# Second wide attention layer: the first pair's transposed exponentials copied out of PSUM by ScalarE instead of VectorE

## The reference

```
q = rope((decoder_query @ Wq).reshape(B, Sq, 16, 64)) / sqrt(64)
k = rope((encoder_key_value @ Wk).reshape(B, Skv, 16, 64))
v = (encoder_key_value @ Wv).reshape(B, Skv, 16, 64)
scores = einsum('bqhd,bkhd->bhqk', q, k);  scores = where(mask, scores, -1e9)
attn = softmax(scores);  out = einsum('bhqk,bkhd->bqhd', attn, v).reshape(B, Sq, 1024) @ Wo
x = decoder_query + out;  then a layer norm of x
```

## Time and profile before

| what | us |
|---|---|
| median of 3 runs | 2019.13 (2017.56 to 2023.05) |
| the profiled execution's own time | 2018.0 |
| its span in the trace | 2016.1 |

### The profile page before, as it was taken

One profiled execution on the slowest core, in us unless ns is written; L12 is line 12 of the kernel. 1 busy time (PEld: TensorE's weight loads), 2 busy tenths in 40 slices (PEclk: granted clock), 3 DMA queues, 4 the chain that ended last, 5 costly groups with the idle time before them and its releaser, 6 DMA issues. The chain is left out here.

```text
span 2016.1 us, 50639 instructions
## 1 busy us (share of the span) xinstructions
PE 1899.3 (94%) x18654; PEld 1644.1 (82%) x18654; DVE 1443.3 (72%) x3163; ACT 1291.5 (64%) x3129; POOL 598.3 (30%) x740
## 2 busy tenths in 40 slices
PE   7799998999999999999999999999999998898998
PEld 6677777898888888888887887887888877777786
DVE  5688875546555555555589899999999974677775
ACT  4577776556656565566566666666666663777775
POOL 3233230000000000000076677777776730000000
PEclk8899999999999999999999999999999997999999
DMA  5444442201101001000102000000100002443441
GB/s 159 151 148 142 125 134 68 92 25 61 28 21 28 17 22 29 21 24 21 42 25 59 20 20 26 23 23 18 30 22 19 22 14 69 126 128 120 128 134 56
DMA packets 111774, 123.02 MB, mean 61 GB/s; under 512 B 45964, under 2 KB 101420, under 8 KB 111532
## 3 DMA queue, kind: packets, MB, share of 16 engines
q1 hardware_dynamic: 111244, 119.26, 20.0%
q10 hardware_dynamic: 288, 0.51, 0.1%
HBM read 82.29 MB, written 37.45 MB: 59 GB/s over the span
## 5 line engine op out<-in xcount | busy, mean ns | idle before, releaser
L645 ACT ACTIVATE L_P<-PS,MX 100x361 f32<-100x361 f32 x512 | 252.6, 565 | 126.8 <-DVE MX L775 126.8
L775 DVE TENSOR_REDUCE MX<-PS 100x2 f32<-100x722 f32 x256 | 219.9, 901 | 52.9 <-PE PS L525 52.7
L537 PE MATMUL PP<-CON,L_P 100*128 100x100 f32 x1536 | 180.8, 254 | 26.7 <-DVE L_PT L782 22.1
L1544 ACT ACTIVATE wide_V<-PJ 105x512 f32<-105x512 f32 (+1 forms) x143 | 84.1, 594 | 165.5 <-PE PJ L1375 165.5
L1579 ACT ACTIVATE wide_P<-wide_P,MX 100x361 f32<-100x361 f32 x256 | 149.9, 588 | 59.6 <-DVE MX L1717 57.8
L537 PEld LDWEIGHTS PP<-CON,L_P 100*128 100x128 f32 x1536 | 148.5, 142 | 47.4 <-ACT L_P L645 33.9
L1579 ACT ACTIVATE wide_P<-PS,MX 100x361 f32<-100x361 f32 x256 | 140.4, 563 | 70.0 <-DVE MX L1722 70.0
L1442 PEld LDWEIGHTS PS<-CON,wide_P 100*128 100x128 f32 x1536 | 159.6, 140 | 29.4 <-ACT wide_P L1579 8.1
L1442 PE MATMUL PS<-CON,wide_P 100*128 100x100 f32 x1536 | 176.9, 250 | 4.1 <-ACT wide_P L1579 3.1
L1938 POOL TENSOR_TENSOR wide_AC<-wide_T,wide_COSM 128x362 f32<-128x362 f32 x128 | 133.2, 1041 | 155.2 <-issue 155.2
L1455 PEld LDWEIGHTS PP<-wide_PT,wide_V 128*64 128x64 f32 (+1 forms) x3072 | 137.0, 137 | 38.1 <-issue 38.0
(11 more groups left out here) (252 smaller groups left out, 5627.2 us busy)
## 6 DMA issues: line engine op xcount, KB each, us to landing
strips<-L_KS SPq DMA_DIRECT2D x256, 90.5 KB
L_KA<-strips SPq DMA_DIRECT2D x64, 362.0 KB, 3.1
wide_RB<-recip SPq DMA_DIRECT2D x128, 100.0 KB, 2.8
C<-ctx_t SPq DMA_DIRECT2D x32, 361.0 KB, 3.1
kept<-L_CTH SPq DMA_DIRECT2D x16, 361.0 KB, 4.8
kept<-L_CTL SPq DMA_DIRECT2D x16, 361.0 KB, 5.4
L_CTH<-kept SPq DMA_DIRECT2D x16, 361.0 KB, 4.2
L_CTL<-kept SPq DMA_DIRECT2D x16, 361.0 KB, 5.0
```

The source lines that it names most:

```text
L537: last = nc.tensor.transpose(PPB[:, n, SQ * t:SQ * t + SQ], P[:, (4 * g + 2 * i + n) % 8, 128 * t:128 * t + 128], ident[0:SQ, 0:SQ])
L645: nc.scalar.activation(P[:, (4 * g + j) % 8, 0:SK], PSB[0:SQ, j, 0:SK], ACT.Exp, bias=MX[:, s % 2, 4 * q + j:4 * q + j + 1], scale=1.0).th ...
L775: nc.vector.tensor_reduce(MX[:, s % 2, 4 * q + 2 * i:4 * q + 2 * i + 2], PSB[0:SQ, 2 * i:2 * i + 2, 0:SK], AX.X, ALU.max, negate=True).the ...
L1544: nc.scalar.activation(V[0:r, 1024 * t + 512 * part:1024 * t + 512 * part + 512], bank(key)[0:r, 0:512], ACT.Copy).then_inc(Z["v_taken"], 1)
```

## The change

In layer 2 (slots of `s >= B`) the copy of the first pair's transposes leaves VectorE and is made by ScalarE, right behind its two copies of K tiles to `wide_T` and ahead of the second `wide_KH`. Layer 1 keeps its division. Each copy still counts up the semaphore that TensorE waits for, `unloaded_first` for the first pair.

```diff
                         act.wait_ge(Z["turned"], 2 * g + 2)
                         if g >= 4:
                             act.wait_ge(Z["weighed"], g - 1)
-                        nc.scalar.activation(PT[:, 2:4, :], PSB[:, 2:4, 0:KV_TILES * SQ], ACT.Copy).then_inc(Z["unloaded_second"], 1)
+                        n = 2 * (g % 2)
+                        nc.scalar.activation(PT[:, n:n + 2, :], PSB[:, n:n + 2, 0:KV_TILES * SQ], ACT.Copy).then_inc(unloaded(g)[0], 1)
@@ ScalarE's loop over slots @@
                         for key in first:
                             job(key)
+                        if B <= s < NS:
+                            unload(2 * G)
                         for key in turns_of(G - 1)[1:]:
                             rotated_high(key)
@@ VectorE's loop over slots @@
                         for key in first:
                             job(key)
-                        if s < NS:
+                        if s < B:
                             unload(2 * G)
```

## The result

The changed kernel took 2011.84 us in the median of 11 runs (2006.65 to 2016.52), the kernel before 2020.17 (2014.8 to 2029.46, 11 runs). The ratio is 0.9957, 95% interval 0.9941 to 0.9972: faster by 0.4%, where I had forecast 2021.5, no change or slower. Two executions of later runs, at 6086 and 4449 us, were far off all others of their kernels and are left out of the ratios. The profiled execution has a span of 2014.0 us.

A forecast was written before the change was run, and what follows sets the result against it. TensorE, nearly full with VectorE close behind, was taken to bound the kernel; VectorE's relief counted nothing, and ScalarE's lateness 0.35 us a period times 7.0 added 2.5 us, giving 2021.5 us, own range 2017.5 to 2027, one-in-ten limits 2011 to 2034.

The forecast's parts named there:

- What bounds: Layer 2's repeating stretch: TensorE and VectorE close to full, busy 524.1 and 511.6 of 550 us; ScalarE a third idle.
- At most 1.9 us a period: TensorE's waits behind VectorE: 1.0 + 0.2 + 0.4 + 0.3 us per 78.3 us period, the most VectorE's lateness costs.
- TensorE's idle 3.4 us a period: TensorE in layer 2: the most a change leaving its own list alone can give back, 25.9 us in the stretch.
- VectorE's side: VectorE's wide_KL after losing the copy: 0.68 us saved, 0.5 becomes waiting for ScalarE; between nothing and 0.2 us a slot.
- The term that I put at nothing: VectorE's 0.2 us left per slot, taken as zero because GpSimd's products were said to set the first wide_KL's length.
- my upper end: VectorE's 0.2 us counted at three TensorE waits on wide_T: 0.6 us a period, 4 us in all.
- The rule of the Trainium skill: Two-input VectorE and GpSimd instructions lock each other out of shared SBUF ports; read as gain zero, otherwise 4 us kept.
- ScalarE's side: Added copy delays the second pair's copy by 0.57 us; slots 2 and 3 late, mostly absorbed, 0.35 us a period left.
- Rival 2's second form: Half of the 13.3 us from VectorE's waits gained, with ScalarE's lateness against it: 2012.5 us.
- the whole rival: VectorE's relief pays: the 1.9 us of waits a period go, 13.3 us less, 2006, or half, 2012.5; chance 0.17.
- Rival 1's mechanism: ScalarE's lateness in slots 2 and 3 not absorbed: 1.5 us a period, 10.4 us in all, 2029.5; chance 0.28.
- The marks I set: Changed profile: VectorE busy down 49 us, wide_KL waits 25 us or more, wide_QL wait stays 1.13, period within 0.9 of 78.3.

The follow-up runs named there:

- the relieved kernels: Kernel before with VectorE's first-pair copy put between the two wide_KL, or left out on both engines: periods 75.48 and 75.42 us against 78.37.
- the faster version: Kernel before, VectorE's copy between the two wide_KL, GpSimd's wide_QL behind the first K tile's two products: ratio 0.9854, median 1986.92 us, period 74.28.
- the narrowed one: Kernel before with GpSimd's two products of every K tile cut from 362 columns to 2 (output wrong): ratio 0.9795, period 72.94 us.
- order-only kernel: Kernel before, VectorE keeping its first-pair copy but behind the first wide_KL instead of ahead of both; ScalarE untouched: ratios 0.992 and 0.991.
- no copy anywhere: Kernel before with layer 2's first-pair copy left out on both engines, TensorE not waiting for it (output wrong): ratio 0.991, period 75.42 us.
- five sixths of the gain from slots 2 and 3: Kernel before with VectorE's copy between the two wide_KL in slots 2 and 3 alone: ratio 0.9944, period 75.95 us.
- held back: Changed kernel, VectorE's first wide_KL of a layer 2 slot waiting until ScalarE has copied the second K tile to wide_T: ratio 1.001, period 78.32 us.
- a control run: Kernel before plus an unneeded ScalarE copy into a scratch tile, 300 columns where 600 were meant; VectorE keeps its own: ratio 1.0008, period 78.28 us.
- both narrowed kernels: Kernel before and changed kernel, each with GpSimd's two products per K tile cut from 362 columns to 2: ratios to before 0.9795 and 0.9836.

## Why the prediction was wrong, by its own steps

- **What bounds.** That both TensorE and VectorE bind was right. The two ceilings were too low. "At most 1.9 us a period" lies behind VectorE, I said; the relieved kernels gained 2.9. And TensorE's idle 3.4 us a period was to be all that can come back; the faster version gained 4.1, and the narrowed one 5.4. I had taken TensorE's busy time as fixed. Six periods, before and in the faster version:

```profile
1109.81:1580.00 470.19, 449.46 (x3913) 386.34 (x3912) 437.30 (x1148) 312.53 (x848) 337.99 (x409) 1.00 0.09 23
1109.85:1555.55 445.70, 440.64 (x3907) 386.15 (x3906) 396.08 (x1143) 312.36 (x843) 334.10 (x408) 1.00 0.10 24
```

  That is 74.9 us of busy time a period before and 73.4 after, for the same products: of the 4.1 us, 2.6 were idle time and 1.5 recorded as busy. In the order-only kernel the 2.9 us divide into 1.8 and 1.1. Why the busy time shrinks is not shown; a record of TensorE may hold time in which it waited.
- **VectorE's side: the step that failed.** I worked out 0.2 us left per slot, then took nothing, on the ground that GpSimd's products set the length of wide_KL. The 0.2 was there (2.76 to 2.56 in the slot I looked at, 2.62 to 2.39 in the mean), but partly by luck: I had halved 2.17 us into 1.08 each where the two took 0.96 and 1.29, and the second one's 1.07 afterwards is set by where it meets a product. The products do set the length of what meets them, and for that very reason the first wide_KL, which now starts before them, is freed: 0.51 us instead of 0.96. The term that I put at nothing was worth 2.9 us a period by itself (no copy anywhere), and 1.16 are left of it beside ScalarE's added copy. Nor may a relief be counted once per wait of TensorE, as my upper end did (0.6 us a period). My reading is that slots 2, 3 and 0 follow each other with VectorE late throughout, so what each saves adds up until TensorE's next wait; five sixths of the gain from slots 2 and 3 fits this, and no run tests it alone. That VectorE's end decides is shown both ways: 1.001 with the old end (held back), 0.992 with an earlier end and nothing moved (order only).
- **The rule of the Trainium skill.** I read the port lock as "the copy was free time for GpSimd, so nothing is gained" and let it decide. The lock is there (527 ns without GpSimd's products, 1094 with them), but whose turn comes first decides what it costs, and moving the copy changed the turn.
- **ScalarE's side.** The place and size were right: waits for wide_PT of 0.3, 0.5 and 0.3 us in the slots named, against 0.49, 0.58 and 0.33 worked out, and nothing in total as long as VectorE is late (period 78.32 against 78.37 in the held-back kernel). What I missed is the coupling: with VectorE relieved they are what bounds the period, 1.8 us of it.
- **The rivals.** Rival 2's second form, half of the waits with ScalarE's lateness against it, gave 2012.5; 2011.84 was measured. It names the two sides rightly, and its number is close by luck: 2.9 less 1.8 us a period, not half of 1.9. I had given the whole rival 0.17, with the argument that the second wide_KL is tied to ScalarE. The tie is real (58.1 us of waits) and did not decide. Rival 1's mechanism, ScalarE's lateness not absorbed once VectorE is no longer late, is the 1.8 us (1.5 by my sum), but it came on top of a larger gain.
- **The marks I set.** The wait of wide_KL for wide_KH came, larger than forecast (58 us for 25 or more); VectorE's busy time fell by 75.5 instead of 49 us, the first sign that something besides the copy had gone; the wait before the scores for wide_QL, which was to stay, fell from 1.13 to 0.84; and the period moved by 1.16 us, past the 0.9 that I had named.

Not tried: ScalarE's copy of the full 600 columns added to the kernel before with VectorE keeping its own; and whether the second wide_KL of the changed kernel could be freed as well without delaying ScalarE's copies to wide_T.

## What to carry to other kernels

Where VectorE and GpSimd both work on SBUF, look at the spread of an instruction's length before its count. One that takes 0.5 us at best and 1.1 in the median may be waiting for the other engine, which the time line of both shows; here a copy out of PSUM, as long beside GpSimd as without it, was the one to place where they would meet. Before moving work to another engine, try the other order on the same engine: here that gave twice the gain and no late ScalarE. The busiest engine's busy time was no floor: TensorE's fell from 74.9 to 73.4 us a period with the same products. When two engines are both late ahead of a third, price each alone and both together; they don't add. And look up in the trace what a control run did: the extra copy of one had half of the columns meant.

## What the runs showed of the hardware

- A subtraction of 128 x 362 float32 with both inputs in SBUF takes 509 to 539 ns on VectorE with GpSimd's long products cut (both narrowed kernels), and up to 1306 ns beside them. Each of the 112 in the kernel before (1066 to 1616 us) began inside a product and ended 0.39 to 0.40 us behind the product's end.
- It goes the other way as well: a GpSimd product of 128 x 362 takes 818 ns at least, and the 112 that began inside a wide_KL of the kernel before ended 0.68 to 0.83 us behind that wide_KL's end.
- A VectorE copy of 128 x 600 out of PSUM took 0.77 us beside a GpSimd product, as without one (751 to 785 ns in all 64 of the kernel before, 750 to 783 in all 64 with GpSimd's long products cut).
